# A Mamba block's output projection taken from full-precision products to three products of rounded halves, for five of its eight groups

## What is computed

```
x = x + xattn(layernorm(x), ctx)
h = layernorm(x)                       # 128 tokens x 512
gate, hBC, dt = h @ in_proj_w.T        # 8192 + 10240 + 128 columns
hBC = silu(conv4(hBC) + conv_b)        # x, B, C; x is 128 heads of 64
y = ssd(x, B, C, softplus(dt + dt_bias), A) + D * x
y = y * rsqrt(mean(y*y) + eps) * norm_w * silu(gate)
x = x + y @ out_proj_w.T               # 8192 -> 512: the output projection
x = x + ffn(x)
```

## Time and profile before

| | us |
|---|---|
| median of 3 runs | 656.05 |
| the profiled execution's own time | 655.37 |
| its span | 653.6 |
| PE busy | 623.4 (95%) |
| DVE busy | 437.6 (67%) |
| ACT busy | 340.7 (52%) |
| POOL busy | 209.4 (32%) |

### The profile page before, as it was taken

The page is one execution under the profiler, slowest core; times in us unless marked ns, Lnnn a source line. Parts: engine busy times, 40 slices in busy tenths (PEclk is TensorE's granted clock), DMA queues, the critical chain, the costliest instruction groups (busy, mean ns, idle before and its releaser), DMA issues. The chain is left out here.

```text
span 653.6 us, 11055 instructions
## 1 busy us (share of the span) xinstructions
PE 623.4 (95%) x3938; PEld 532.2 (81%) x3938; DVE 437.6 (67%) x889; ACT 340.7 (52%) x615; POOL 209.4 (32%) x159
## 2 busy tenths in 40 slices
PE   7999999899999999999997679998999999999998
PEld 6888888799999989999996579987778788797573
DVE  3532144777777777777777356978975957758873
ACT  3413114668676867687765433675354444537210
POOL 0000000458676857686762244022220220200000
PEclk9999999999999999999999799998999999999999
DMA  7501013376777677776667958483757668597600
GB/s 254 212 0 33 1 65 77 91 198 181 189 188 186 181 189 186 187 186 178 163 154 183 272 249 227 188 322 129 252 206 256 254 202 310 198 360 293 244 1 16
DMA packets 30301, 118.64 MB, mean 182 GB/s; under 512 B 7936, under 2 KB 8320, under 8 KB 22704
## 3 DMA queue, kind: packets, MB, share of 16 engines
q1 hardware_dynamic: 29296, 116.01, 56.9%
q10 hardware_dynamic: 960, 2.03, 1.1%
HBM read 86.30 MB, written 0.26 MB: 132 GB/s over the span
## 5 line engine op out<-in xcount | busy, mean ns | idle before, releaser
L1563 PEld LDWEIGHTS ps<-norm_t,ring 128*128 128x128 f32 x1152 | 132.7, 193 | 4.9 <-issue 4.1
L1563 PE MATMUL ps<-norm_t,ring 128*128 128x128 f32 x1152 | 134.2, 277 | 0.0
L482 POOL TENSOR_TENSOR pt_lo<-far_t,pt_hi 128x512 fp32r<-128x512 f32 x84 | 99.3, 1199 | 66.6 <-ACT pt_hi L582 66.6
L1159 DVE SCALAR_TENSOR_TENSOR acc<-raw,cw,acc 128x127 f32<-128x127 f32 (+2 forms) x240 | 85.0, 430 | 24.7 <-ACT acc L795 24.0
L997 DVE TENSOR_SCALAR_CACHE_REDUCE prob_far<-ps 128x1024 f32<-128x1024 f32 x64 | 73.4, 1149 | 19.7 <-PE ps L1330 18.1
L659 ACT ACTIVATE prob_far<-prob_far,neg_max 128x1024 f32<-128x1024 f32 x64 | 69.9, 1092 | 23.4 <-DVE neg_max L1001 23.3
L582 ACT ACTIVATE pt_hi<-far_t 128x512 fp32r<-128x512 f32 x96 | 53.5, 590 | 50.7 <-PE ps L1330 49.7
L1025 DVE STREAM_TRANSPOSE prob_far<-prob_far 128x1920 f32<-128x1920 f32 x32 | 69.4, 2172 | 0.3 <-ACT prob_far L659 0.2
L1328 PE MATMUL ps<-k_hi,q_hi 128*128 128x512 f32 (+2 forms) x160 | 62.3, 390 | 4.4 <-DVE q_lo L902 1.6
L1328 PE MATMUL ps<-pt_hi,v_hi 128*128 128x256 f32 x208 | 61.1, 294 | 3.3 <-DVE pt_lo L902 3.3
L557 POOL TENSOR_SCALAR_AFFINE_SELECT at_hi<-a_hi 128x2048 fp32r<-128x2048 f32 x8 | 16.1, 2014 | 139.5 <-PE ps L1575 128.0
(11 more groups left out here) (206 smaller groups left out, 1217.6 us busy)
## 6 DMA issues: line engine op xcount, KB each, us to landing
ring<-w_in_dram SPq DMA_DIRECT2D x36, 1024.0 KB, 4.9
far_t<-prob_far SPq DMA_DIRECT2D x248, 120.0 KB, 2.3
ring<-w_out_dram SPq DMA_DIRECT2D x16, 1024.0 KB, 4.9
ring<-wq_dram SPq DMA_DIRECT2D x16, 512.0 KB, 4.3
ring<-wo_dram SPq DMA_DIRECT2D x16, 512.0 KB, 3.6
w_sb<-w_dram SPq DMA_DIRECT2D x4, 896.0 KB, 9.1
ring<-ctx_t_dram SPq DMA_DIRECT2D x3, 1024.0 KB, 5.0
ring<-w_dram SPq DMA_DIRECT2D x3, 1024.0 KB, 7.8
```

Source lines behind the costliest of these rows:

```text
L482: sub = lambda dst, a, hi: pool.tensor_tensor(dst, a, hi, ALU.subtract)
L1159: ins = nc.vector.scalar_tensor_tensor(a[:, i, back:], r[:, i, 0:T - back], cw[:, bass.ds(tile + i, 1), 3 - back:4 - back].rearrange("p a ...
L1563: ins = mm(ps[:, bank, t * T:t * T + T], w[:, t, c, :], norm_t[:, c, :], start=(c == 0), stop=(c == NC - 1))
```

## The change

For groups 0 to 4 (`ROUNDED = 5`) the output projection is made as `split_product` of rounded halves. ACT rounds each chunk of `w_out` (`out_round`, 128x2048, into `out_hi[i]`) and the gated values (`gated_round`, 128x1024, into `ug_hi`). POOL subtracts to get the chunk's low half (`out_low`, 128x2048, into `ring_lo`, which lies in the ring slot itself). DVE subtracts to get `ug_lo` (`gated_low`, 128x1024). PE waits on `ugl_ok` and `outl_ok` and makes 24 products a group in place of 8. Groups 5 to 7 keep float32. The loops of DVE and PE over steps 3 to 6 are written out; ACT's loop over steps 1 to 4 stays, with the added work inside. The new tiles lie where other tiles are not in use, so no memory is added.

```diff
@@ gpsimd
+            def out_low(g, i):
+                slot = out_chunk(g, i)[0]
+                pool.wait_ge(outh_ok, 2 * g + i + 1)
+                sub(ring_lo[slot][:].rearrange("p (t n) -> p t n", t=4), ring[slot][:].rearrange("p (t n) -> p t n", t=4),
+                    out_hi[i][:].bitcast(F32)).then_inc(outl_ok, 1)
+
             for g in range(GROUPS - 2):
+                if 0 < g <= ROUNDED:
+                    out_low(g - 1, 0)
+                    out_low(g - 1, 1)
                 pool.wait_ge(seg_ps, 2 * g + 4)
                 steps_a(g + 2)
@@ scalar
+            def out_round(g, i):
+                slot, before = out_chunk(g, i)
+                act.wait_ge(landed[slot], (before + 1) * 16)
+                copy(out_hi[i][:], ring[slot][:].rearrange("p (t n) -> p t n", t=4)).then_inc(outh_ok, 1)
+
+            def gated_round(g, b):
+                act.wait_ge(ug_ok, 2 * g + 2)
+                copy(ug_hi[b][:], ug[b][:]).then_inc(ugh_ok, 1)
...
             copy(c2_st[:], c2_sb[:]).then_inc(c2h_ok, 1)
+            gated_round(0, 0)
+            out_round(0, 0)
...
-            def mamba_step(g, b, last=False):
+            def mamba_step(g, b, split_out, split_next, last=False):
                 k, o = 2 * g + 6, 1 - b
                 decay_exp(g + 1, o, 0)
+                if split_out:
+                    out_round(g - 1, 1)
                 raw_out(step_chunk(g, 0), k, 0, 8 * g + 8)
...
                 gate_out(step_chunk(g, 2), 0, sg[o][:, 0:4, :])
                 if last:
                     w1_split(2)
+                if split_next:
+                    gated_round(g, b)
+                    out_round(g, 0)
                 gate_out(step_chunk(g, 3), 1, sg[o][:, 4:8, :])
...
             with act.Fori(0, 2) as turn:
                 for i in range(2):
-                    mamba_step(turn * 2 + (i + 1), 1 - i)
-            mamba_step(5, 1)
-            mamba_step(6, 0, True)
+                    mamba_step(turn * 2 + (i + 1), 1 - i, True, True)
+            mamba_step(5, 1, True, False)
+            mamba_step(6, 0, False, False, True)
@@ vector
+            def gated_low(g, b):
+                dve.wait_ge(ugh_ok, g + 1)
+                sub(ug_lo[b][:], ug[b][:], ug_hi[b][:].bitcast(F32)).then_inc(ugl_ok, 1)
...
             add_squares(0)
+            gated_low(0, 0)
...
                 gate(g, b)
                 add_squares(g)
+                if g < ROUNDED:
+                    gated_low(g, b)
@@ tensor
+            def split_out_proj(g, b, i, first=False):
+                slot = out_chunk(g, i)[0]
+                pe.wait_ge(ugl_ok, g + 1)
+                pe.wait_ge(outl_ok, 2 * g + i + 1)
+                w_lo_ = ring_lo[slot][:].rearrange("p (t n) -> p t n", t=4)
+                for t in range(4):
+                    ins = split_product(ps[:, 6, :], ug_hi[b][:, 4 * i + t, :], ug_lo[b][:, 4 * i + t, :],
+                                        out_hi[i][:, t, :], w_lo_[:, t, :], first and i == 0 and t == 0, False)
+                ins.then_inc(freed[slot], 1)
...
-                out_proj(before_g, 1 - b, 0, first)
-                out_proj(before_g, 1 - b, 1)
+                for i in range(2):
+                    if before_g < ROUNDED:
+                        split_out_proj(before_g, 1 - b, i, first)
+                    else:
+                        out_proj(before_g, 1 - b, i)
```

More of the change, by code:

```diff
@@ L78 @@
 LN_STEPS = 8
+ROUNDED = 5
 WARM = 12
@@ L230, in build @@
                 sq_tok = sbuf(st4, "sq_tok", [P, 2, T])
-                ug = [sbuf(st4, f"ug{b}", [P, TPG, T]) for b in range(2)]
+                ug, ug_lo = [], []
+                for b in range(2):
+                    with ExitStack() as same_place:
+                        ug_lo.append(sbuf(same_place, f"ug_lo{b}", [P, TPG, T], F32R))
+                    ug.append(sbuf(st4, f"ug{b}", [P, TPG, T]))
                 at_hi.append(sbuf(st4, "at_hi1", [P, HPG, T], F32R))
@@ L236, in build @@
                     w1_lo = sbuf(same_place, "w1_lo", [P, NC, FF], F32R)
+                with ExitStack() as same_place:
+                    out_hi = [sbuf(same_place, f"out_hi{i}", [P, 4, DM], F32R) for i in range(2)]
+                    ug_hi = [sbuf(same_place, f"ug_hi{b}", [P, TPG, T], F32R) for b in range(2)]
                 w1_sb = sbuf(st4, "w1_sb", [P, NC, FF])
@@ L283, in build @@
         ug_ok, var_s = sem("ug_ok"), sem("var_s")
+        outh_ok, outl_ok, ugh_ok, ugl_ok = sem("outh_ok"), sem("outl_ok"), sem("ugh_ok"), sem("ugl_ok")
         f_mask = sem("f_mask")
@@ L1229, in _ @@
             add_squares(0)
+            gated_low(0, 0)
             def mamba_step(g, b):
                 q, k, o = 4 * g + 8, 2 * g + 6, 1 - b
-                if not (isinstance(g, int) and g == 1):
+                if g > 1:
                     x_times_dt(g)
@@ L1241, in mamba_step @@
                 add_squares(g)
[L1243 to L1247, removed]
+                if g < ROUNDED:
+                    gated_low(g, b)
+            for g in range(1, GROUPS - 1):
+                mamba_step(g, g % 2)
             def w1_split(c):
@@ L1594, in y_product, with out_proj @@
                 ins.then_inc(y_ps, 1)
-            def out_proj(g, b, i, first=False, last=False):
+            def out_proj(g, b, i, last=False):
                 slot, before = out_chunk(g, i)
@@ L1602, in out_proj @@
                 for t in range(4):
-                    ins = mm(ps[:, 6, :], ug[b][:, 4 * i + t, :], w[:, t, :], start=(first and i == 0 and t == 0),
+                    ins = mm(ps[:, 6, :], ug[b][:, 4 * i + t, :], w[:, t, :], start=False,
                              stop=(last and i == 1 and t == 3))
+                ins.then_inc(freed[slot], 1)
[7 more added lines that the diff above has]
+                                        out_hi[i][:, t, :], w_lo_[:, t, :], first and i == 0 and t == 0, False)
                 ins.then_inc(freed[slot], 1)
@@ L1639, in mamba_step @@
                 project(g, 1)
-                out_proj(before_g, 1 - b, 0, first)
-                out_proj(before_g, 1 - b, 1)
+                for i in range(2):
[3 more added lines that the diff above has]
+                        out_proj(before_g, 1 - b, i)
                 project(g, 2)
                 project(g, 3)
[L1645 to L1649, removed]
+            for g in range(1, GROUPS - 1):
+                mamba_step(g, g - 1, g % 2, g == 1)
             x_transposes(7, 1)
```

## The result

The changed kernel takes 673.26 us (median of 4 runs, 672.54 to 674.1), against 655.66 for the kernel before in runs on the same chip: a ratio of 1.0269, 95% interval 1.0252 to 1.0286. The execution that was profiled took 672.54 us with a span of 670.7. Over that span the mean granted clock of TensorE is 0.977.

What follows compares the result with a forecast made beforehand. PE's own work bound the kernel at 26.0 us a step; POOL and DVE excluding each other make it 29.7. The end comes 24 us late: 655.37 becomes 679.4, plus 0.7 to the median, 680 us; range 670 to 688.

Steps and rivals of the forecast that it cites:

- PE: Output projection: products of halves take 5.60 us for 6.87, a gain of 1.27 us a step, 6.3 in five steps.
- ACT's order and the first wait: Start of step 1: copies queued ahead of the first `decay` make it late, and PE waits 3.7 us.
- POOL's subtraction: `out_low` on POOL: a 128x2048 subtraction takes 4.60 us, from the slope of two smaller rows.
- The hold, and the mask: DVE instructions with two SBUF operands, masks included, can't run beside POOL's: 13.2 and 13.3 us a step, together 26.5.
- The sign that I had named: In the profile after: single taps or masks of 4 to 5 us beside POOL's subtraction.
- The loop: From one step's `gate` end to the next, through ACT, POOL and DVE: 29.7 us in place of 26.0.
- the seam: Between POOL's two subtractions: the mask of the first half goes in there, 1.2 us.
- The sum: `gate` of step 5 ends at 603.2, 29.3 us late; step 6 starts 24.0 late, and so does the end.
- B: Rival: POOL holds only the taps, not the masks, 1.2 us less in each of five steps: 674 us; chance 0.12.
- A: Rival: POOL's subtractions leave DVE alone, the step is PE's 24.7 us: 653.5 us; chance 0.06.
- C: Rival: PE's idle time keeps its clock low and PE joins the loop, 2 us more a step: 688 us; chance 0.09.
- C's sign: In the profile after: PE has no wait for `xc`, where the forecast had about 3 us a step.

Runs made afterwards that it cites:

- experiment 5: Experiment 1 with ACT's `ug_hi` moved behind the first `decay`, `gated_low` behind the first mask, `out_hi` of chunk 0 between the two `sg`: 647.97 us, ratio 0.9897.
- experiment 1: The changed kernel with POOL's subtractions cut to one column, the low half of `w_out` left out of the sum: 654.69 us, ratio 0.9989.
- experiment 2: The changed kernel with each POOL subtraction replaced by three memsets that read nothing, the low half left out: 654.47 us, ratio 0.9981.
- experiment 4: The changed kernel with ACT's `out_hi` of chunk 0 put ahead of `ug_hi`, nothing else: 671.31 us, ratio 1.0257.
- experiment 7: The changed kernel with the moves of experiment 5 and the subtraction left on POOL, everything computed: 668.92 us, ratio 1.0207.
- experiment 8: Experiment 6 with POOL's `c_st` subtraction (16 partitions, 4 us) in step 5 in place of step 1: 654.86 us, ratio 0.9988.
- experiment 6: Experiment 3 with the moves of experiment 5, everything computed: 654.88 us, ratio 0.9992.
- experiment 3: The changed kernel with `out_low` on DVE in place of POOL, everything computed: 659.3 us, ratio 1.0079.

## Why the prediction was right, and where it was off

The verdict (slower, 94%) was right. 673.3 us lies inside 670 to 688, and 6.7 below the 680 forecast. By its steps:

- **PE.** 5.67 us where I had 5.60. Right, and experiment 5 shows what it is worth with nobody in its way: a steady step of 24.6 us for 26.0.
- **ACT's order and the first wait.** 3.63 us measured, 3.7 forecast. Right. I had given the low clock behind it no price; in experiment 1 it is at most 2.6 us. In the changed kernel it is covered, as DVE is later still: what counts there is G of step 1, the end of its `gate`.
- **POOL's subtraction.** 4.60 taken; the first of the two in step 3 takes 4.54. The 4497 ns that the prediction took from the Trainium skill's page "GPSIMD Engine Reference" are as near; they stand in its section "Elementwise — side-by-side cycle accounting", for an addition, and not in the section that the prediction named.
- **The hold, and the mask.** Right: a mask in the middle of a subtraction takes 2.85 us, taps 3.71 and 2.08. The sign that I had named, single ones of 4 to 5 us, was set too high: a mask or tap comes in the middle of a subtraction and waits for the rest of it, and the longest beside one in step 5 are these 2.85 and 3.71. Experiments 1 and 2 show the cause by taking it away in two ways, and 4 and 7 by moving it to other instructions of the same kind.
- **The loop.** The structure is what was forecast, and a size was off: 29.7 us against 28.47. Term by term, from the rows of step 5 above (G = 565.27 + 2.19 = 567.46):

| term | forecast | measured |
|---|---|---|
| G to POOL's start | 3.1 | 570.44 - 567.46 = 2.98 |
| two subtractions and the mask's seam | 10.4 | 580.40 - 570.44 = 9.96 |
| AFFINE_SELECT pair | 4.0 | 4.07 |
| taps behind it | 2.7 | 2.49 |
| `skip_add` and the gap ahead | 2.4 | 2.22 |
| mask | 1.1 | 1.13 |
| twelve taps and the gap behind | 3.7 | 593.74 - 590.31 = 3.43 |
| gate | 2.2 | 2.19 |
| sum | 29.7 | 28.47 |

  No term is missing; five are 0.1 to 0.4 us too long. What was mis-sized is the list from "POOL's first subtraction 4.60: 7.7" to "gate 0.39 + 2.19: 29.7". Its largest error is the seam: I gave the mask there its whole 1.2 us, and the two subtractions with it take 9.96 - 2 x 4.54 = 0.88 us more than by themselves. The rest is that I mostly took full printed durations and added gaps, though the rows overlap (the mask starts at 589.18, before the 587.11 + 2.16 of the `skip_add` ahead of it), and that the gap ahead of `gate` was 0.22 us and not 0.39.
- **The sum.** `gate` of step 5 ends at 593.74 + 2.19 = 595.93, forecast 603.2, so 7.3 us earlier: 4 x 1.22 = 4.9 from the loop, 1.0 from step 1 (32.3 us from `gate` to `gate`, forecast 33.3), and 1.4 that this execution was ahead before step 1 began (444.29 against 445.71; over the other profiles this start lies between 443.69 and 446.74). Step 6 starts at 594.30, forecast 577.28 + 24.0 = 601.3, and the rest of the kernel takes 78.2 us where it took 78.1.
- **The rivals.** B gave 674 and a step of 28.5, and the measured time and step landed on them, but by accident: B was a mask that isn't held, and the mean of line 1211 is 1766 ns where it was 1221, with 2.85 and 3.33 us for single ones. The 1.2 us of a step come from the sizes in the table. A is refuted by the rows and by experiments 1 and 2, yet its arithmetic nearly holds: 653.5 for a POOL that leaves DVE alone, 654.7 and 654.5 in these two. C's sign did show in part, as PE has no wait for `xc` ahead of steps 5 and 6. But the clock (0.94 over step 5) doesn't set the step: PE's slower matmuls only fill time in which it had waited for `xc` in step 3, and the step is 28.5 us in both. C's 688 didn't come.

What stays open: why, in experiments 4 and 7, two orders that differ come to the same 27.7 us. The shared time of POOL and DVE is a lower bound that I worked out at 26.5 us; what makes up the last 1.2 wasn't taken apart.

## What to carry to other kernels

Before work is given to an idle engine, look for a row that shows it beside the busy one: an instruction that takes far longer than elsewhere (one tap of 4133 ns here, where twelve take 3.21 us) and ends when the other engine's instruction ends shows the price, which is up to the whole duration of the helper's instruction. Then follow the loop from the last producer to the next, with distances between starts in place of printed durations, as durations overlap. An engine whose own work fills the step (24.54 of 24.65 us for DVE in experiment 8) has no room left: what is put on it once stays as a lag. Here that decided which groups were worth changing: 654.9 us with all five, 650.8 with four.

## What the runs showed that I had not expected

- Who is kept out depends on who runs back to back. Between two POOL instructions one DVE instruction gets in; four DVE instructions in a row let none of POOL's in (`at_hi` 7.04 us for 2.0 of work, experiment 6).
- DVE does the same fp32 subtraction of 128x2048 in 2.29 us where POOL needs 4.54 (the Trainium skill's page "GPSIMD Engine Reference", section "Elementwise — side-by-side cycle accounting", has 2293 and 4497 ns for an addition of 2048 fp32 elements), and with it there the step falls from 28.5 to 25.3 us (experiment 3), though it is more work on the busier engine.
- POOL's memsets hold nothing: twelve taps take 3.22 us beside them.
- Where PE had waited 3.67 us, up to 454.78, the clock granted from 454 to 462 us was 0.58. That step was 5.1 us longer than with a wait of 1.16 us at that place and 1.00 granted, though PE idled only 1.1 us more in it; 1.4 us of the difference lie ahead of the wait (experiments 1 and 5).
